# Generated self-attention of a sixteen-batch decoder: queries, keys and results held on 256 packed rows, with copies within SBUF between these rows and the head groups

## The reference, cut to what matters

```python
def _gen_param(sub, Wl, W, Bp):
    p = jnp.einsum('a...,a->...', sub, Wl[0])
    return jnp.tanh(p) * W + Bp
...
def _block(hs, ln1_g, ln1_b, ln2_g, ln2_b, *p):
    ca, cp, cf, cm = (p[0:8], p[8:16], p[16:24], p[24:32])
    b_, s_, d_ = hs.shape
    h = _layernorm(hs, ln1_g, ln1_b)
    qkv = _student_linear(h, *ca)
    q, k, v = jnp.split(qkv, 3, axis=-1)
    split = lambda t: t.reshape(b_, s_, H, HD).transpose(0, 2, 1, 3)
    q, k, v = (split(q), split(k), split(v))
    scores = jnp.einsum('bhqd,bhkd->bhqk', q, k) / float(HD) ** 0.5
    causal = jnp.tril(jnp.ones((s_, s_), dtype=bool))
    scores = jnp.where(causal, scores, jnp.asarray(-10000.0, scores.dtype))
    attn = jax.nn.softmax(scores, axis=-1)
    o = jnp.einsum('bhqk,bhkd->bhqd', attn, v)
    o = o.transpose(0, 2, 1, 3).reshape(b_, s_, d_)
    o = _student_linear(o, *cp)
    hs = hs + o
```

## Time and profile before

| | us |
|---|---|
| median of three runs | 3742.02 |
| lowest, highest | 3741.71, 3757.2 |
| the profiled execution, total | 3767.73 |
| its span in the trace | 3765.9 |
| TensorE busy in the span | 3224.3 (86%) |
| VectorE, ScalarE, GpSimd busy | 1817.5, 1205.8, 904.1 |
| `L3Self`: first instruction of VectorE to last | 2930.39 to 3125.4 |

### The profile page before, as it was taken

One profiled execution on the slowest core, in us unless ns is written; L12 is line 12 of the kernel. 1 busy time (PEld: TensorE's weight loads), 2 busy tenths in 40 slices (PEclk: granted clock), 3 DMA queues, 4 the chain that ended last, 5 costly groups with the idle time before them and its releaser, 6 DMA issues. The chain is left out here.

```text
span 3765.9 us, 77622 instructions
## 1 busy us (share of the span) xinstructions
PE 3224.3 (86%) x31312; PEld 2218.8 (59%) x31312; DVE 1817.5 (48%) x4553; ACT 1205.8 (32%) x2374; POOL 904.1 (24%) x736
## 2 busy tenths in 40 slices
PE   7886999999986875879657899869998899999978
PEld 2333445544566773556634555559997786566655
DVE  7886443344134342452267666643333663355543
ACT  1222222222213332221131656522222462244433
POOL 1000432243000000221633878712111210104000
PEclk9888999999998986989878999979999899999989
DMA  4212000000115011341631111058887200021100
GB/s 149 65 56 81 15 9 8 16 8 0 48 35 39 4 23 29 99 116 42 210 101 30 32 28 33 10 180 336 326 326 268 83 13 12 28 72 50 47 9 15
DMA packets 173794, 287.14 MB, mean 76 GB/s; under 512 B 79105, under 2 KB 144071, under 8 KB 164148
## 3 DMA queue, kind: packets, MB, share of 16 engines
q1 hardware_dynamic: 166004, 262.37, 22.6%
q0 software_dynamic: 7488, 20.46, 1.6%
HBM read 244.37 MB, written 28.48 MB: 72 GB/s over the span
## 5 line engine op out<-in xcount | busy, mean ns | idle before, releaser
L2581 PE MATMUL ps<-L_ffn_xsT,arena 128*128 128x128 f32 x2584 | 315.8, 282 | 32.4 <-DVE L_ffn_xsT L2397 19.7
L2581 PEld LDWEIGHTS ps<-L_ffn_xsT,arena 128*128 128x128 f32 x2584 | 307.2, 198 | 36.6 <-DVE L_ffn_xsT L2397 22.6
L161 POOL TENSOR_TENSOR rstd<-nsc,mhalf 112x4 f32<-112x4 f32 (+1 forms) x24 | 40.1, 1669 | 956.3 <-DVE nsc L154 955.4
L793 POOL TENSOR_TENSOR L_xattn_rn<-L_xattn_ss,mhalf 125x16 f32<-125x16 f32 (+1 forms) x64 | 185.7, 2901 | 324.5 <-DVE L_xattn_ss L847 324.5
L3254 POOL TENSOR_TENSOR L_xattn_pT<-L_xattn_pT,L_xattn_keep 125x678 int32<-125x678 int32 x128 | 190.5, 1510 | 71.8 <-ACT L_xattn_pT L3509 71.8
L686 PE MATMUL ps<-L_attn_prod,arena 128*32 128x448 f32 (+31 forms) x672 | 157.3, 538 | 44.9 <-DVE L_attn_prod L508 44.9
L2489 ACT ACTIVATE L_ffn_silu<-ps,arena 128x128 f32<-128x128 f32 x280 | 102.9, 368 | 269.4 <-PE ps L2581 253.6
L961 PE MATMUL ps<-arena,L_xattn_cT 128*125 128x512 f32 x384 | 170.3, 596 | 4.3 <-DVE L_xattn_unit L840 4.3
L2406 DVE SCALAR_TENSOR_TENSOR L_ffn_hT<-ps,arena,L_ffn_silu 128x128 f32<-128x128 f32 x280 | 98.0, 351 | 155.7 <-ACT L_ffn_silu L2489 155.7
L508 DVE TENSOR_TENSOR L_attn_prod<-arena,L_attn_k 128x448 f32<-128x448 f32 (+10 forms) x336 | 160.5, 546 | 2.3 <-PE ps L686 2.3
L2278 POOL DMA_INDIRECT L_ffn_rows_out<-L_ffn_ys,L_ffn_dest x78 | 80.0, 1026 | 339.4 <-DVE L_ffn_ys L2415 304.2
(11 more groups left out here) (576 smaller groups left out, 6780.6 us busy)
## 6 DMA issues: line engine op xcount, KB each, us to landing
arena<-in_L_ffn_up SPq DMA_DIRECT2D x35, 2056.0 KB, 8.0
arena<-in_L_ffn_down SPq DMA_DIRECT2D x35, 1152.0 KB, 8.3
L_xattn_ctxT<-in_ctxT SPq DMA_DIRECT2D x48, 375.0 KB, 3.6
arena<-in_L_ffn_up SPq DMA_DIRECT2D x43, 384.0 KB
L_attn_a<-L_attn_skew SPq DMA_DIRECT2D x16, 784.0 KB, 5.5
L_xattn_ctx<-in_ctx SPq DMA_DIRECT2D x30, 375.0 KB
arena<-L_xattn_kp SPq DMA_DIRECT2D x64, 93.8 KB, 3.3
L_xattn_mask<-in_mask SPq DMA_DIRECT2D x32, 164.1 KB, 8.4
```

What stands on the lines that cost most here:

```text
L793: nc.gpsimd.tensor_tensor(rn[0:r, i], ss[0:r, i], core.mhalf[0:r, 0:H], ALU.pow).then_inc(po_r.step("root", i), 1)
L2581: ins = nc.tensor.matmul(ps[:, 2 + b % 4, half * TS:(half + 1) * TS], self.up(i % WU, k, half * HM + m), xsT[:, i % 2, k], start=(k == 0), ...
```

## The change

Queries, keys and results are kept on 256 rows (two tiles of 128), in the order group, feature, tile, so that the 64 rows of one group of four heads are contiguous. The padded weights and the padded output weights go away.

- `product` makes queries and keys from 8 matmuls (L4632 after) instead of 16. They land interleaved in `packed`.
- SP's `placed(n)` copies them to the head groups in `qk` with four transfers of 64 runs of 896 bytes (L4375), and `scores(n)` waits for those. `results(n)` copies the sums to `den` (16 runs of 448 bytes, L4383) and the results to `op` (four transfers of 64 runs of 448 bytes, L4385).
- `denominators` and `widened` are gone. `inverses` now waits for the transfers, and inverts a tile of 16 partitions x 112 (L4468). `spread` is two matmuls with `of_head` (L4670) and waits for the inverse; `divided` and `project` work on two tiles.
- The order on the engines is changed: queries and keys run three batches ahead instead of two, the transposes four; on VectorE `inverses(i-1)` stands behind `shifted(i+1, 1)`, in front of `queries(i+3)`. `scores(i+1)` on TensorE now also waits for the queries and keys of i+2 to have left PSUM.
- The prefetch is cut in three parts of seven, seven and six transfers, which SP issues in i = 0, 1 and 2 behind `placed(i+3)`; `late` follows in i = 9. `prepared` runs one or two iterations later.
- The bias of the output is computed once as a full tile, and GpSimd adds it to `y` (`biased`). In the stage in front (`L2Experts`) one wide add, a small add and a memset become one plain add.

```diff
             def scores(n):
-                ten.wait_ge(ve_q.sem, ve_q.at(n, "q"))
-                ten.wait_ge(ac_k.sem, ac_k.at(n, "k"))
+                ten.wait_ge(qk_in[n % 2], (n // 2 + 1) * HQ * DMA)
                 for j in range(NQ):
                     for g in range(HQ):
-                        r, at = slice(g * Z, (g + 1) * Z), slice(j * T, (j + 1) * T)
-                        ins = nc.tensor.matmul(ps[0:T, g, at], q[r, n % 2, at], k[r, n % 2, at], start=True, stop=True)
+                        r = slice(g * Z, g * Z + HD)
+                        ins = nc.tensor.matmul(ps[0:T, g, j * T:(j + 1) * T], both(qk, n)[r, j, 0, :], both(qk, n)[r, j, 1, :], start=True, stop=True)
...
         @block.sync
         def _(sp):
-            run.prefetch(sp)
...
+            def placed(n):
+                sp.wait_ge(ve_q.sem, ve_q.at(n, "q"))
+                sp.wait_ge(ac_k.sem, ac_k.at(n, "k"))
+                if n >= 2:
+                    sp.wait_ge(pe_s.sem, pe_s.at(n - 2, "scores"))
+                for g in range(HQ):
+                    sp.dma_start(qk[g * Z:g * Z + HD, n % 2].rearrange("p (j t) -> p j t", j=NQ),
+                                 both(packed, n)[g % 2 * 64:(g % 2 + 1) * 64, g // 2].rearrange("p i t -> p (i t)")).then_inc(qk_in[n % 2], DMA)
+
+            def results(n):
+                sp.wait_ge(ac_p.sem, ac_p.at(n, "o"))
+                if n >= 2:
+                    sp.wait_ge(ve_d.sem, ve_d.at(n - 2, "divided"))
+                by_tile = lambda t: t.rearrange("p (j t) -> p j t", t=T)
+                sp.dma_start(den[:, n % 2], by_tile(o[0:128:Z, n % 2])).then_inc(o_in[n % 2], DMA)
+                for g in range(HQ):
+                    sp.dma_start(op[g % 2 * 64:(g % 2 + 1) * 64, n % 2, g // 2 * T:(g // 2 + 1) * T],
+                                 by_tile(o[g * Z + 1:g * Z + 1 + HD, n % 2])).then_inc(o_in[n % 2], DMA)
+
+            sem, arena = run.ahead
+            share = -(-len(arena.loads) // 3)
+            for n in range(3):
+                placed(n)
+            for i in range(NB):
+                if i >= 1:
+                    results(i - 1)
+                if i + 3 < NB:
+                    placed(i + 3)
+                for dst, src in arena.loads[i * share:(i + 1) * share]:
+                    sp.dma_start(dst, src).then_inc(sem, DMA)
+                if i == 9:
+                    for n, src in following.late:
...
             def inverses(n):
-                dve.wait_ge(pe_r.sem, pe_r.at(n, "den"))
+                dve.wait_ge(o_in[n % 2], (n // 2 + 1) * (HQ + 1) * DMA)
...
-                nc.vector.reciprocal(inverse[:, n % 2], ps[0:T, 3, 0:H]).then_inc(ve_r.step("inverse"), 1)
+                nc.vector.reciprocal(inverse[:, n % 2], den[:, n % 2]).then_inc(ve_r.step("inverse"), 1)
...
             for i in range(NB):
                 if i + 1 < NB:
                     shifted(i + 1, 0)
-                if i >= 1:
-                    inverses(i - 1)
                 if i >= 2:
                     update(i - 2, 0)
                 if i + 1 < NB:
                     shifted(i + 1, 1)
-                if i + 2 < NB:
-                    queries(i + 2)
-                if i + 4 < NB:
-                    front(i + 4)
+                if i >= 1:
+                    inverses(i - 1)
+                if i + 3 < NB:
+                    queries(i + 3)
+                if i + 5 < NB:
+                    front(i + 5)
...
             def spread(n):
-                ten.wait_ge(ac_r.sem, ac_r.at(n, "wide"))
-                for j in range(NQ):
-                    ins = nc.tensor.transpose(ps[:, 7, j * T:(j + 1) * T], wide[:, j * 128:(j + 1) * 128], core.ident[0:T, 0:T])
+                ten.wait_ge(ve_r.sem, ve_r.at(n, "inverse"))
+                for m in range(KD):
+                    ins = nc.tensor.matmul(ps[:, 7, m * T:(m + 1) * T], self.of_head[:, m * 128:(m + 1) * 128], inverse[:, n % 2], start=True, stop=True)
...
             for i in range(NB):
                 if i + 1 < NB:
                     if i == 0:
-                        ten.wait_ge(bias, 1)
-                    if i >= 2:
-                        ten.wait_ge(ve_r.sem, ve_r.at(i - 2, "inverse"))
+                        ten.wait_ge(bias, 2)
+                    if i + 2 < NB:
+                        ten.wait_ge(ve_q.sem, ve_q.at(i + 2, "q"))
+                        ten.wait_ge(ac_k.sem, ac_k.at(i + 2, "k"))
...
                 if i + 1 < NB:
                     ten.wait_ge(ac_s.sem, ac_s.at(i + 1, "scores", 1))
-                if i >= 1:
-                    if i + 1 == NB:
-                        ten.wait_ge(ve_r.sem, ve_r.at(i - 2, "inverse"))
-                    denominators(i - 1)
-                if i + 2 < NB:
-                    queries(i + 2)
-                    keys(i + 2)
+                if i + 3 < NB:
+                    queries(i + 3)
+                    keys(i + 3)
                 attend(i)
                 if i + 2 < NB:
                     values(i + 2)
-                if i + 3 < NB:
-                    turn(i + 3, 6)
+                if i + 4 < NB:
+                    turn(i + 4, 6)
                 if i >= 1:
                     spread(i - 1)
```

191 lines of the change are left out of this document (95 added, 96 removed).

## The result

The changed kernel takes 3754.57 us (median of 20 runs, 3746.7 to 3764.04). The kernel before, run beside it, takes 3745.8 (20 runs, 3739.31 to 3757.2). The ratio is 1.002, with a 95% interval of 1.0012 to 1.0028: some 7.5 us slower, where -1.0 us was forecast. The time itself lies in the range, and within 0.5% of no change, but the kernel became slower and not a little faster. One of the ten runs of the kernel `early` further down (6008.13 us) and one of the kernel before beside it (5610.03 us) were slow and are in no ratio.

What follows compares the result with a forecast made beforehand. TensorE's list of 11.27 us an iteration was taken as the bound, then a 9.12 us softmax loop. Scores -0.3 (27.0 us of stalls included), tail -1.0, ramp +0.3 gave -1.0 us: 3741, own range 3728 to 3756, 8-in-10 range 3714 to 3768.

Steps and rivals of the forecast that it cites:

- Softmax loop sets the pace, 9.12 us: Steady iteration: scores to reciprocal 7.77, reciprocal 0.83, semaphore 0.05 and spread 0.47 close a loop of 9.12 us.
- GpSimd's added add ... I cost at nothing: One add a batch on GpSimd, off both loops, priced at zero because GpSimd is busy 7.47 of 40 us.
- `bend` and the preparation, at nothing too: ScalarE's bend and the shorter preparation in L2Experts, priced at zero; if uncovered, below 1 us a batch.
- Halved and dropped matmuls, TensorE 7.83: TensorE's list per iteration falls from 11.27 to 7.83 us: queries and keys -1.87, projection -0.86, denominators -0.71.
- The second loop, through SP: Reciprocal, queries, placed transfers and results through SP's queue take 8.8 us, hidden under 9.12 by 0.3 us only.
- Prefetch stalls of 10.1, 6.0, 1.1 and 4.8: Results queued behind weights stall iterations 0, 1, 2 and 9 by these us; with clock 27.0 us together.
- The clock: Granted clock 0.50 behind a long stall, costing 0.6 us more in the spread and 1.0 in the next scores.
- Tail -1.0: From the scores of batch 14 to the end of the last update: about 1.0 us shorter.
- 5.0, and a longer reciprocal, in the place of ... some 4: Tail: last results cost five issues and a landing, 5.0 us, plus longer reciprocal, replacing denominators, widening and waits, some 4.
- No stall, 3714: Rival at the prefetch: results pass the weights or land early, so the gain stays, -28 us; chance 0.16.
- SP's queue at 12.5 us: Rival: SP's queue sets the pace at 12.5 us an iteration, +41 us, 3782; chance 0.15.
- third case: VectorE's or ScalarE's work later, loops up to 0.5 us longer, or ramp 5 us: +5 to +12; within the forecast's 0.66.

Runs made afterwards that it cites:

- early: first_pebias with reciprocal and queries moved ahead of the second half of the shift on VectorE; ratio to the kernel before 0.9978, stage 190.9 us.
- no_add: Changed kernel without GpSimd's addition of the projection's bias to y, so the output lacks that bias; stage 204.5 us, one run.
- first_pebias: Changed kernel with results sent before placed transfers and weights, and the bias added by one more matmul instead of GpSimd; ratio to before 0.9979, stage 191.1 us.
- early_only: Changed kernel with only reciprocal and queries moved ahead of the second half of the shift on VectorE; stage 207.7 us, one run.
- first_split: Changed kernel with results sent first and the six large loads issued two to an iteration in three iterations; ratio to before 0.9963, stage 186.6 us.
- tail_fill: Changed kernel with useless matmuls in TensorE's gaps in the last two batches alone; stage 199.2 us, tail 32.5 us, one run.
- results_first: Changed kernel with each batch's results sent before the next placed transfers and the weights; ratio to before 0.9974, stage 190.1 us.
- act_queue: Changed kernel with the weights of i = 0, 1, 2 issued from ScalarE's queue, SP's order kept; stage 200.6 us, one run.
- fill: Changed kernel with five useless matmuls ahead of each spread on TensorE; stage 203.5 us, one run.

## Why the prediction was wrong, point by point

Two steps of the prediction failed. The sum of the tail had no term for the granted clock (3.9 us) and too small a one for the last results, and GpSimd's addition was costed at nothing, where it sets 0.33 us of each undisturbed distance. The forecast for the stalls erred by 3.7 us the other way.

- **Softmax loop sets the pace, 9.12 us.** Right in kind, 9.50 in size. The term that failed is "GpSimd's added add ... I cost at nothing". It was priced by GpSimd's idle time, but it runs beside VectorE's subtraction, which is on the loop, and lengthens it from 1.09 to 1.42. Without it the distance is 9.17 (`no_add`). The text named this as a way to be wrong and left it out of the sum. Counted in each of the thirteen distances it is 0.33 x 13 = 4.3 us. That is bookkeeping: in no run did the stage give them back when the add went (`no_add` 204.5 against 203.8, `first_pebias` 191.1 against 190.1).
- **`bend` and the preparation, at nothing too.** Two distances of the middle are above 9.50 at full clock. In the one of 9.78 GpSimd's mask takes 2.20 and not 1.93 us; it starts at 3022.61, when VectorE is still preparing weights (from 3020.69, 2.33 us). In the one of 9.92 ScalarE copies the scores 1.71 us after they start and not 1.30, behind its `bend` (3029.94, 1.92 us). Together these distances are 0.7 us over 9.50.
- **Halved and dropped matmuls, TensorE 7.83.** Right: from start to start the products take 1.86 and the projection 0.87, as forecast. The second loop, through SP, stayed hidden: outside the prefetch and the last batch no reciprocal waits. `early_only` shows how thin its cover is.
- **Prefetch stalls of 10.1, 6.0, 1.1 and 4.8.** Right in place and mechanism: 8.56, 6.14, 0 and 3.02. Counted from the scores of batch 1, results(0) and (1) were forecast for 25.5 and 42.3, and their reciprocals start at 24.8 and 41.7. In the distances, (17.94 + 16.97 + 10.99 + 13.35 + 11.54) - 5 x 9.50 = 23.3 us with the clock behind them, against 27.0. `first_split` shows that 17.2 us of the stage can be had by the order and the portions of the transfers alone. The Trainium skill, page "DMA: Bandwidth & Descriptors", section "Specifications", says that a read-modify-write is made below 512 B. By the medians it does not show here: the 28 KB transfers of the earlier trace rows, in runs of 448 B, landed in 2.4 us on the median, and the 56 KB of L4375, in runs of 896 B, in 2.3.
- **The clock.** I took it as 1.00 outside the long stalls. It also fell once in the steady loop, where TensorE is idle for 1.4 to 1.9 us an iteration, and before the change for at most 0.5: 1.6 us in the distance of 11.13. It fell for longer in the tail.
- **Tail -1.0.** The step that failed worst: +4.9. Some 3.9 us are the clock (`tail_fill`), which the sum of this part did not contain at all, although I had priced it for the stalls: the tail is the place with the longest gaps on TensorE outside the prefetch, 2.91 and 3.71 us. The transfers did what was said (from the issue at 3100.83 to the reciprocal at 3105.68 are 4.85 us, forecast 5.0), but the step on the last results was too small. Before, and then after:

```profile
3118.43 0.53 ACT L4559 COPY L_attn_o<-ps 128x448 f32<-128x448 f32 x1
...
3121.68 0.55 PE L4647 MATMUL ps<-ident,L_attn_wide 112*128 112x112 f32 x4
```

```profile
3093.27 1.19 PE L4670 MATMUL ps<-L_attn_inverse,arena 16*128 16x112 f32 x4 [2.91 <-DVE L_attn_inverse L4468]
...
3100.28 0.53 ACT L4596 COPY L_attn_o<-ps 128x448 f32<-128x448 f32 x1 [1.70 <-PE ps L4663]
...
3106.57 1.19 PE L4670 MATMUL ps<-L_attn_inverse,arena 16*128 16x112 f32 x4 [3.71 <-DVE L_attn_inverse L4468]
```

From the end of ScalarE's copy to the last spread pass 5.8 us (3100.81 to 3106.57) against 2.7 before (3118.96 to 3121.68), 3.0 more, where "5.0, and a longer reciprocal, in the place of ... some 4" makes 1.6. The last 0.6 us are in the last full iteration: 9.73 from scores to scores where 9.12 was forecast.

- **The rivals.** "No stall, 3714" did not come true, nor did SP's queue at 12.5 us. The +8.8 lie in the third case's +5 to +12. Its longer loops came true, with 0.38 us, but its costly ramp did not (+0.3), and the clock of the tail, 3.9 us of the sum below, is not in it. That the number lies there is in part luck.

Against me stand the add with 4.3 us, the clock of the tail with 3.9, the last results with 1.4, the clock, `bend` and the mask in the middle with 2.3; in my favour the stalls with 3.7. That is 8.2 of the 9.8 us between -1.0 and +8.8. Of the other 1.6, 0.6 are the last full iteration, and most of the rest is that the undisturbed distances forecast as 7.9, 8.85 and 9.12 were each a little longer than that with the add counted.

## What to carry to other kernels

Price an instruction on an idle engine by what runs beside it on the critical engine, not by the idle time. When a change takes the bound away from TensorE, the remaining chain can pay twice, by its waits and by the lower clock on what is left; price that in the tail first, where the waits are longest. A small transfer that an engine waits for goes ahead of the weights in its queue, and the weights go in portions that fit under one iteration: the same change is then 0.26% (`results_first`) to 0.37% (`first_split`) faster than before instead of 0.2% slower. When a kernel with such falls of the clock is compared with another from one trace each, look first whether a fall stands in one of them and not in the other.

## What the runs showed of the hardware

- VectorE's subtraction of 112 x 896 took 1.42 us beside GpSimd's addition of 112 x 256 and 1.09 without it. GpSimd's mask, which overlaps the first reduction (2993.50 to 2994.39), left that at 1.09 against 1.07 for the second. The mask itself took 2.14 to 2.20 us in the three iterations in which it started before VectorE's preparation of 2.27 or 2.33 us had ended, and 1.92 to 1.94 in the others.
- Issuing is not of one price: a small transfer took 0.43 us to issue on SP in a quiet time, and two of 4 KB took 3.76 us (changed kernel) and 4.50 us (`act_queue`) with several MB outstanding. ScalarE did nothing else for 7.83 us while it issued.
- With TensorE idle for about 1.5 us in each 9.5, the granted clock fell to 0.50 in one stretch of some 7 us of the steady loop in the changed kernel and not at all in `tail_fill` (58.01 us at 1.00). With useless matmuls in most of that gap it was 1.00 throughout (58.07 us in `fill`). In the tail, where the gaps are 2.91 and 3.71 us, filling them brought steps of 3.23 and 2.05 us down to 1.75 and 1.03.
- The results' 448 B runs needed 9.5 us from last issue to landing behind large loads in the same queue, and 6.2 beside large loads in another queue, against the 2.4 of the earlier trace rows.
